# Second edge stage of a graph network: the product of aggregate and x moved from the rows before the transposes to the turned rows behind them, with new orders on three engines

## The reference, cut to what matters

```
agg = segment_sum(x[src] * w, dst)
L0  = leaky(x*agg @ W1 + b1) + leaky(agg @ W2 + b2);  L0 = L0 / |L0|
x   = layernorm(x + L0)
msg = gelu(gelu(x[dst] @ W1p + b1p) @ W2p + b2p) * w      # per edge
agg = segment_sum(msg, src)                                # second aggregate
x   = layernorm(x + normed FFN of [x, agg])
```

## Time and profile before

| | |
|---|---|
| median of three runs | 2975.88 us |
| the profiled execution's own time | 2982.28 us |
| its span | 2980.5 us |
| granted TensorE clock, mean | 0.767 |
| busy, share of the span | PE 72%, DVE 74%, ACT 36%, POOL 79% |
| second edge stage, first gather to last scatter | 1273.0 to 2578.3 us |

### The profile page before, as it was taken

The page is one execution under the profiler, slowest core; times in us unless marked ns, Lnnn a source line. Parts: engine busy times, 40 slices in busy tenths (PEclk is TensorE's granted clock), DMA queues, the critical chain, the costliest instruction groups (busy, mean ns, idle before and its releaser), DMA issues. The chain is left out here.

```text
span 2980.5 us, 39234 instructions
## 1 busy us (share of the span) xinstructions
PE 2150.9 (72%) x11956; PEld 1675.4 (56%) x11956; DVE 2211.5 (74%) x5627; ACT 1070.7 (36%) x1964; POOL 2361.0 (79%) x1774
## 2 busy tenths in 40 slices
PE   4036555555555554269999999989999998599997
PEld 3035555555554544247777666666666666366664
DVE  5079888888888886457778777777777777188888
ACT  0000000000000000035555455545555554288887
POOL 7777888888888888758888888888888887488888
PEclk8555555555555555579999999999999999699998
DMA  9998888888888767467787777777777776356664
GB/s 228 206 204 187 180 173 177 175 183 177 176 180 170 158 141 151 83 175 179 186 187 184 169 166 176 180 176 159 178 178 169 170 175 123 79 196 207 206 209 156
DMA packets 1036087, 516.48 MB, mean 173 GB/s; under 512 B 540544, under 2 KB 998336, under 8 KB 1035880
## 3 DMA queue, kind: packets, MB, share of 16 engines
q1 hardware_dynamic: 764616, 372.57, 47.6%
q0 software_dynamic: 144256, 77.17, 19.2%
q10 hardware_dynamic: 127008, 64.23, 7.6%
HBM read 269.97 MB, written 243.84 MB: 172 GB/s over the span
## 5 line engine op out<-in xcount | busy, mean ns | idle before, releaser
L300 PE MATMUL sums<-xg,weigh 128*128 128x64 f32 x1960 | 437.7, 420 | 514.8 <-ACT ms L323 358.7
L546 POOL DMA_INDIRECT state<-ms,sidx x392 | 630.8, 1609 | 145.2 <-issue 116.9
L256 POOL DMA_INDIRECT table<-ms,sidx x392 | 622.2, 1587 | 142.2 <-issue 115.5
L300 PEld LDWEIGHTS sums<-xg,weigh 128*128 128x128 f32 x1960 | 423.2, 329 | 548.6 <-issue 471.5
L368 DVE TENSOR_SCALAR weigh<-rowp,key,ew 128x128 f32<-128x128 f32 (+3 forms) x784 | 423.9, 602 | 167.9 <-PE rowp L288 160.7
L532 POOL DMA_INDIRECT box<-table,node_dst x392 | 401.9, 1025 | 130.0 <-issue 107.6
L243 POOL DMA_INDIRECT xg<-in_x,node_src x392 | 382.8, 976 | 120.8 <-issue 104.9
L323 ACT ACTIVATE ms<-sums 128x256 f32<-128x256 f32 x98 | 37.6, 384 | 1144.4 <-DMA table<-ms,sidx 1076.1
L374 DVE SCALAR_TENSOR_TENSOR seen<-rowp,key,earlier 128x128 f32<-128x128 f32 (+3 forms) x784 | 383.1, 544 | 0.0
L579 PE MATMUL z_p<-turned_s,wz 128*128 128x512 f32 x588 | 331.7, 647 | 24.9 <-ACT turned_s L652 20.8
L589 PE MATMUL o_p<-cenz,leaky 128*128 128x65 f32 x2352 | 285.1, 278 | 27.6 <-DVE leaky L737 27.2
(11 more groups left out here) (94 smaller groups left out, 3549.6 us busy)
## 6 DMA issues: line engine op xcount, KB each, us to landing
box<-table SPq DMA_DIRECT2D x97, 768.0 KB, 5.3
joins<-weigh ACTq DMA_DIRECT2D x98, 640.0 KB, 3.8
weigh_in<-joins SPq DMA_DIRECT2D x98, 640.0 KB
table<-rows SPq DMA_DIRECT2D x97, 512.0 KB, 5.4
pair<-state SPq DMA_DIRECT2D x97, 512.0 KB, 3.8
xin<-in_x SPq DMA_DIRECT2D x97, 256.0 KB, 6.1
state<-y SPq DMA_DIRECT2D x97, 256.0 KB, 7.7
out<-y SPq DMA_DIRECT2D x97, 256.0 KB, 2.2
```

Source lines behind the costliest of these rows:

```text
L256: pool.indirect_dma_start(out=table[:, :], out_offset=bass.IndirectOffsetOnAxis(ap=sidx[0][:, i:i + 1], axis=0), in_=ms[k % MR][:, b, :], ...
L300: last = pe.matmul(sums[k % 2][:, a * D:(a + 1) * D], block_of(0, k, b)[:, a * P:(a + 1) * P], xg[:, k * WT + b, :], start=b == a, stop=b ...
L546: pool.indirect_dma_start(out=state[:, :], out_offset=bass.IndirectOffsetOnAxis(ap=sidx[1][:, at:at + 1], axis=0), in_=ms[k % SM][:, b, :] ...
```

## The change

The multiply on the box goes. T now transposes [aggregate, x] straight from the box. E evicts only partitions 0 to 63 (the turned aggregate). A new `multiply(i, q)` on DVE writes partitions 64 to 127 of `turned_s` as turned x (in PSUM) times the evicted aggregate (in SBUF), three times per window with 512 elements each. P waits for it, and T of the tile after next waits for it instead of for the eviction. The step lists of PE, ACT and DVE are ordered anew: T0, T1, E0 and E1 run one round earlier, O one round earlier (at PE's end of the round), `add_rows` one round later (DVE's first step), `turn_neighbours` one round earlier.

```
                         def turn(i, q):
-                            wait(pe, turned_in, n - 1)
+                            wait(pe, multiplied, n - 1)
                             if q == 0:
-                                pe.wait_ge(multiplied, i + 1)
+                                s = i % SB
+                                pe.wait_ge(gathered[s], 16 * WT * (i // SB + 1))
+                                pe.wait_ge(loaded[s], 16 * (i // SB + 1))
...
                         def products(i, q):
-                            pe.wait_ge(turned_in, n + 1)
+                            pe.wait_ge(multiplied, n + 1)
...
 PE      before                    after
-        (2, products, 2)          + (1, products, 0)
-        (5, join)                 + (1, turn, 2)
-        (4, turn_neighbours)      + (1, products, 1)
-        (2, outputs, 0)           + (5, join)
-        (2, outputs, 1)           + (0, turn, 0)
-        (4, first_product)        + (1, products, 2)
-        (1, turn, 0)              + (4, first_product)
-        (1, turn, 1)              + (4, second_product)
-        (1, products, 0)          + (3, turn_neighbours)
-        (1, turn, 2)              + (0, turn, 1)
-        (1, products, 1)          + (1, outputs, 0)
-        (4, second_product)       + (1, outputs, 1)
...
 ACT evict
-   act.activation(turned_s[q][:, :], turned_p[(3 * i + q) % 2][:, :], ACT.Copy).then_inc(turned_in, 1)
+   act.activation(turned_s[q][0:D, :], turned_p[(3 * i + q) % 2][0:D, :], ACT.Copy).then_inc(turned_in, 1)
 ACT     before                    after
-        (5, second_gelu)          + (2, square)
-        (2, slope, 2)             + (1, slope, 0)
-        (5, take)                 + (1, evict, 2)
-        (3, square_centred)       + (1, slope, 1)
-        (4, neighbours_in)        + (0, evict, 0)
-        (2, square)               + (4, neighbours_in)
-        (1, evict, 0)             + (5, take)
-        (4, first_gelu)           + (1, slope, 2)
-        (1, evict, 1)             + (4, first_gelu)
-        (1, slope, 0)             + (4, second_gelu)
-        (1, evict, 2)             + (0, evict, 1)
-        (1, slope, 1)             + (2, square_centred)
...
-                        def multiply(i):
-                            dve.tensor_tensor(box[s][:, :, 1, :], box[s][:, :, 1, :], box[s][:, :, 0, :], ALU.mult).then_inc(multiplied, 1)
+                        def multiply(i, q):
+                            n = 3 * i + q
+                            dve.wait_ge(turned_in, n + 1)
+                            dve.tensor_tensor(turned_s[q][D:2 * D, :], turned_p[n % 2][D:2 * D, :], turned_s[q][0:D, :], ALU.mult
+                                              ).then_inc(multiplied, 1)
 DVE     before                    after
-        (2, sum_outputs)          + (3, add_rows)
-        roots(t)                  + (1, multiply, 0)
-        (1, leak, 0)              + (1, multiply, 1)
-        (3, normalize)            + (3, sum_centred)
-        (2, scale)                + (2, sum_outputs)
-        (1, leak, 1)              + (1, leak, 0)
-        (2, add_rows)             + (1, multiply, 2)
-        (1, leak, 2)              + roots(t)
-        (2, sum_centred)          + (1, leak, 1)
-        (0, multiply)             + (2, scale)
-                                  + (3, normalize)
-                                  + (1, leak, 2)
```

More of the change, by code:

```diff
@@ L633, in _ @@
                         for t in range(ROUNDS):
-                            of(t, 2, products, 2)
-                            of(t, 5, join)
-                            of(t, 4, turn_neighbours)
-                            of(t, 2, outputs, 0)
-                            of(t, 2, outputs, 1)
-                            of(t, 4, first_product)
-                            of(t, 1, turn, 0)
-                            of(t, 1, turn, 1)
                             of(t, 1, products, 0)
@@ L644, in _ @@
                             of(t, 1, products, 1)
+                            of(t, 5, join)
+                            of(t, 0, turn, 0)
+                            of(t, 1, products, 2)
+                            of(t, 4, first_product)
                             of(t, 4, second_product)
+                            of(t, 3, turn_neighbours)
+                            of(t, 0, turn, 1)
+                            of(t, 1, outputs, 0)
+                            of(t, 1, outputs, 1)
                     @block.scalar
@@ L701, in _ @@
                         for t in range(ROUNDS):
-                            of(t, 5, second_gelu)
-                            of(t, 2, slope, 2)
-                            of(t, 5, take)
-                            of(t, 3, square_centred)
-                            of(t, 4, neighbours_in)
                             of(t, 2, square)
-                            of(t, 1, evict, 0)
-                            of(t, 4, first_gelu)
-                            of(t, 1, evict, 1)
                             of(t, 1, slope, 0)
@@ L713, in _ @@
                             of(t, 1, slope, 1)
+                            of(t, 0, evict, 0)
+                            of(t, 4, neighbours_in)
+                            of(t, 5, take)
+                            of(t, 1, slope, 2)
+                            of(t, 4, first_gelu)
+                            of(t, 4, second_gelu)
+                            of(t, 0, evict, 1)
+                            of(t, 2, square_centred)
                     @block.vector
@@ L724, in link @@
                             dve.wait_ge(chain, links)
-                        def multiply(i):
-                            s = i % SB
-                            dve.wait_ge(gathered[s], 16 * WT * (i // SB + 1))
-                            dve.wait_ge(loaded[s], 16 * (i // SB + 1))
-                            dve.tensor_tensor(box[s][:, :, 1, :], box[s][:, :, 1, :], box[s][:, :, 0, :], ALU.mult).then_inc(multiplied, 1)
+                        def multiply(i, q):
[3 more added lines that the diff above has]
+                                              ).then_inc(multiplied, 1)
                         def leak(i, q):
@@ L791, in _ @@
                         for t in range(ROUNDS):
+                            of(t, 3, add_rows)
+                            of(t, 1, multiply, 0)
+                            of(t, 1, multiply, 1)
+                            of(t, 3, sum_centred)
                             of(t, 2, sum_outputs)
+                            of(t, 1, leak, 0)
+                            of(t, 1, multiply, 2)
                             if 2 <= t < NWIN + 3:
                                 roots(t)
-                            of(t, 1, leak, 0)
+                            of(t, 1, leak, 1)
+                            of(t, 2, scale)
                             of(t, 3, normalize)
-                            of(t, 2, scale)
-                            of(t, 1, leak, 1)
-                            of(t, 2, add_rows)
                             of(t, 1, leak, 2)
-                            of(t, 2, sum_centred)
-                            of(t, 0, multiply)
         def last_rows():
```

## The result

The changed kernel takes 3131.62 us (median of 4 runs, 3126.90 to 3136.25), the kernel before 2975.23 on the same chip: ratio 1.0518, 95% interval [1.0504, 1.0531]. The forecast was 2977 us with a range of 2962 to 2996, so the time lies far outside it, and none of the three rivals comes near it. The profiled execution took 3126.9 (its span 3125.2).

What follows compares the result with a forecast made beforehand. POOL was taken to bound the second edge stage. The 31 us it would regain go into a fill longer by 12 and a ring longer by 0.8 a round, no longer hidden: 2977 us, range 2962 to 2996.

Steps and rivals of the forecast that it cites:

- three rivals: POOL stays the bound: 2963 us, chance 0.31; DVE meets POOL's hold: 2995, 0.24; POOL isn't freed: 2985, 0.05.
- POOL freed: Second edge stage: without the multiply on the box, POOL loses its 31 us of lengthened scatters and gathers.
- M2 on the ring: DVE's third new multiply lies on the ring: 0.68 us long, a step of 0.60 a round.
- the ring: Compute chain through the single `o_p`, from one O to the next: 12.02 us a round before, 12.82 forecast.
- The holds: DVE's moves to partitions 64 to 127 and back, at M2 and `roots`, add 0.20 us to the ring.
- The fill: Start of the second edge stage, up to the first scatter: 12.3 us longer, first scatter at 1343.8 us.
- PE's path hidden: PE's new order takes 12.1 us a round, under 12.82, so it hides in the wait for `add_rows`.
- the fall of the granted clock: Sign that the forecast is wrong: granted clock under the 1.00 of the earlier trace; no size or chance given.
- TK sets the time, and compute bounds: Stage rounds: the ring (12.82 us) is slower than POOL (12.65), so POOL waits some 0.15 a round for TK.

Runs made afterwards that it cites:

- E0: Not a run: the kernel's step on ACT that evicts tile 0's transposes; no follow-up run has this label, so it has no measured time or ratio.
- e5: Changed kernel's new orders with the old data flow (one multiply in the box, evictions of 128 partitions): 2991.2 us, 1.0038 of the kernel before.
- e11: Kernel before plus three never-read products of 128 x 128 behind the outputs and ahead of F1: 2981.0 us, 1.0007 of the kernel before.
- e12: Kernel before, unchanged, profiled again on the chip of e11: 2975.0 us.
- r_order_alone: e5 run again, unchanged, in another group: 3061.2 us, 1.0194 of the kernel before.
- e2: Changed kernel with tile 1's transposes moved between F1 and F2, and its eviction between the two gelus: 3138.1 us, 1.0526 of the kernel before.
- r_no_hold_m2_short: Changed kernel with all multiplies on partitions 0 to 63, evictions of 128 partitions, and multiply 2 on 8 of 512 columns: 3078.7 us, 1.0284.
- e10: Changed kernel with tile 2's transposes between the output halves, tile 1's between F1 and F2, and three filler products: 3001.8 us, 0.9997.
- r_after: Changed kernel once more, without edits, in another group: 3171.7 us, 1.0595 of the kernel before.
- e4: Changed kernel's new data flow in the old orders, with three multiplies on the ring: 3362.8 us, 1.1213 of the kernel before.

## Why the prediction was wrong

**POOL freed: right.** None of the 784 gathers and scatters of the stage is lengthened (60 before). The means of 1578 and 972 ns are those of the undisturbed round in the earlier trace rows. One input in PSUM leaves POOL alone. The Trainium skill (SBUF, State Buffer, § Who interferes with whom) infers that descriptor generation is spared by a DVE instruction with two SBUF inputs; the 59 to 61 lengthened instructions in the kernel before, e5, e11 and e12 (28 in r_order_alone, where compute is late more often), and 0 in every kernel with the new multiply that was counted, speak against that for indirect DMAs.

**M2 on the ring: right.** 0.69 us for the forecast 0.68.

**The holds: right in kind, too few.** I priced two at 0.20 in all. L0 behind `sum_outputs` and L1 behind the last small one of `roots` are held as well, although no instruction of either pair starts at partition 64: the last reader of PSUM before L0 was M1, before L1 it was M2, and these start at partition 64. That is the rule as the Trainium skill has it (VectorE: DVE Perf Modes, § Two Vector instructions with no wait between them), which compares with the last instruction *in that memory*. I had quoted it so and applied it to neighbours in the list only. The holds come to 0.49, and the ring to 13.02 to 13.06 instead of 12.82: some 20 us.

**The fill: nearly right.** First scatter at 1345.82 us for 1343.8 forecast, +14.3 for +12.3. Counted from the first gather it is 75.2 us for 70.5, since the stage began 2.4 us earlier. The outputs of the fill were slow: 5.36 us in window 2 and 4.77 in window 3.

**PE's path hidden: the step that failed.** "11.4 + 0.7 = 12.1, under 12.82: hidden in the wait for AR" took every duration of PE in the rounds from rows at clock 1.00 and kept them when the waits and PE's order changed. The text named the fall of the granted clock as what would make it wrong, and gave it no price and no chance. It is the largest term by far: 36 of 88 rounds slow, an O of 5.35 for 2.86 us on the ring, 1.3 us a round in the mean, 118 of the 145 us. The kernel before had a sign of it: 0.96 from 1500 to 2500 us. But from window 4 on all its falls came with a wait of PE behind TK, which waited for POOL, and none touched O; I read only the undisturbed stretch of 1.00. When a fall does touch O, PE is busy throughout (8.46 of 8.50 us at 1905.50) and its path is the round: 16.1 us, where 12.1 was to be hidden under 12.82.

**TK sets the time, and compute bounds: right.** TK waited for no scatter in the rounds, POOL waited for TK, 187 us in all, 2.0 a round where 0.15 was forecast.

**What sets off a fall is only partly settled.** Shown: extra work in PE's waits makes it rarer (36 to 12, 33 to 1), in spite of being work; a shorter ring too (36 to 21, 33 to 22). Shown too: the place of the wait between F1 and F2 isn't it (e2). In the kernel before each fall comes with one long wait of PE, 1.8 to 3.6 us; in the changed kernel there are only short ones, up to 0.70 us, and more falls. That fast and slow rounds mostly alternate fits a slow round that leaves PE no wait and a fast one that does, but this is argued, not shown. Not explained: why r_no_hold_m2_short, with fast rounds as short as e5's, has 18 long outputs where e5 has 12; and PE's busy time alone doesn't order the kernels, with 921 of 1000 us in both the kernel before (0.96) and e2 (0.85). Nor is it settled why e5's orders cost 0.4% on one chip and 1.9% on another: ACT's late starts are a part, and their own cause is open.

## What to carry to other kernels

When an edit gives TensorE new waits or a new order, price its rows at the lower clock too: look for stretches at the lower level in the trace of before, see which instructions they cover and what hides them, and ask whether they will still miss the ring. Take an instruction's own duration for that, not the start of the one that waits for it: a late square here was ACT's wait, not a slow O. A DVE instruction that starts on other partitions costs at its return as well, at the next instruction that touches the same memory, wherever in the list that is. If an engine was shielded by a slower one, removing the slower one's burden gains nothing until the shielded engine's stalls are dealt with first: in this kernel the multiply had to be taken off the ring and the clock held up (e10) to come out even.

## What the runs showed of the hardware

More products took less time: three idle products of 128 x 128 in each round gave 64 us back in a program of 3132 us, and six gave 91 in one of 3172, with a granted clock of 0.94 and 0.99 instead of 0.87 from 1500 to 2500 us.

A held DVE instruction starts 0.12 to 0.13 us later, with inputs of 12, 512 or 768 elements, where the earlier trace rows gave 0.20 for 0.11, 0.09 more, on tiny SBUF operations.

Chips differ by up to 28 us in the kernel before (2975 to 3003), and in the profiles of the groups with 2993 to 3003 us the first gather comes about 10 us later:

```profile
1270.58 1.02 POOL L532 DMA_INDIRECT box<-table,node_dst  x1 [2.70 <-POOLq L188]
```

in the profile of after, and in that of r_after

```profile
1282.36 1.02 POOL L532 DMA_INDIRECT box<-table,node_dst  x1 [2.73 <-POOLq L188]
```

so 8 to 13 us of it arise ahead of the stage. Where the rest arises stays open, as no profile of the kernel before on such a chip was made. On these chips ACT also began E0 late in all variants but e4, by 0.27 to 0.88 us in the mean, for 0.04 on the others.
